# The low parts of the second feed-forward's weights are made partly by GpSimd instead of VectorE

## The reference

```python
    def _L1_ffn_ref(x, w_g, c_fc, c_proj):
        ...
        capacity = max(MIN_CAPACITY, int(CAP_FACTOR * N * TOP_K / E))
        xf = x.reshape(N, C)
        logits = xf @ w_g.T
        top_logits, top_idx = jax.lax.top_k(logits, TOP_K)
        router_probs = jax.nn.softmax(top_logits, axis=-1)
        ...
        h = jnp.einsum('ecd,edf->ecf', buf, c_fc)
        h = jnp.square(jax.nn.relu(h))
        expert_out = jnp.einsum('ecf,efd->ecd', h, c_proj)
        ...
    x = x + 0.5 * _L0_ffn_ref(_layernorm(x, axis=-1), ...)
    x = x + _L0_attn_ref(_layernorm(x, axis=-1), ...)
    x = x + 0.5 * _L0_ffn_ref(_layernorm(x, axis=-1), ...)
    x = x + 0.5 * _L1_ffn_ref(_layernorm(x, axis=-1), w_g, c_fc, c_proj)
    x = x + _L1_attn_ref(_layernorm(x, axis=-1), ...)
    x = x + 0.5 * _L1_ffn_ref(_layernorm(x, axis=-1), w_g, c_fc, c_proj)
```

## Time and profile before

| | |
|---|---|
| median of 3 runs | 3040.18 us (3038.32 to 3042.1) |
| the profiled execution's own time | 3041.84 us |
| its span, first to last instruction | 3040.1 us |
| PE busy | 2598.1 us (85%) |
| DVE busy | 2307.1 us (76%) |
| ACT busy | 2223.2 us (73%) |
| POOL busy | 1637.9 us (54%) |

### The profile page before, as it was taken

How to read it: one execution, slowest core, us unless ns; L and a number is a source line. 1 busy time by engine, 2 the same in 40 slices (tenths; PEclk the granted TensorE clock), 3 DMA queues, 4 the chain that set the end, 5 groups by cost and what they waited for, 6 DMA issues and landing times. The chain is left out here.

```text
span 3040.1 us, 42347 instructions
## 1 busy us (share of the span) xinstructions
PE 2598.1 (85%) x12208; PEld 1727.1 (57%) x12208; DVE 2307.1 (76%) x4329; ACT 2223.2 (73%) x2497; POOL 1637.9 (54%) x1288
## 2 busy tenths in 40 slices
PE   7999979999799996999975878778687777589998
PEld 6877756666587774878852323223232232268887
DVE  7677756777566777898977788787787877498887
ACT  5555536656455555777849999999999999777776
POOL 4667642122266763545536676776756667334444
PEclk9999979999899997999976667766666767689999
DMA  3111111111111112111100000000000000021111
GB/s 134 42 56 41 41 23 41 44 43 43 51 42 56 41 41 96 45 43 45 51 0 1 1 1 1 0 1 1 1 1 1 1 1 1 22 92 56 42 55 42
DMA packets 24917, 101.62 MB, mean 33 GB/s; under 512 B 5856, under 2 KB 7904, under 8 KB 15680
## 3 DMA queue, kind: packets, MB, share of 16 engines
q1 hardware_dynamic: 23360, 99.51, 9.5%
q10 hardware_dynamic: 1408, 0.34, 0.0%
HBM read 82.33 MB, written 2.62 MB: 28 GB/s over the span
## 5 line engine op out<-in xcount | busy, mean ns | idle before, releaser
L1911 POOL TENSOR_TENSOR A_Y<-A_Y,A_U 128x2048 f32<-128x2048 f32 x86 | 390.0, 4558 | 222.1 <-ACT A_U L1958 222.1
L1994 DVE TENSOR_SCALAR A_U<-ps 128x1024 f32<-128x1024 f32 x256 | 309.0, 1217 | 127.0 <-POOL A_Y L1911 58.1
L2000 DVE SCALAR_TENSOR_TENSOR A_U<-ps,A_U 128x1024 f32<-128x1024 f32 x256 | 310.8, 1214 | 57.3 <-PE ps L2144 57.3
L2144 PE MATMUL ps<-A_QT,A_KT 9*128 9x512 f32 x512 | 180.8, 702 | 193.6 <-DVE A_U L2000 162.0
L477 POOL TENSOR_TENSOR F0b_h<-F0b_h,dn 128x512 f32<-128x512 f32 x128 | 212.0, 1661 | 111.9 <-DVE F0b_h L409 111.8
L477 POOL TENSOR_TENSOR F0a_h<-F0a_h,dn 128x512 f32<-128x512 f32 x128 | 212.1, 1662 | 104.6 <-DVE F0a_h L409 104.5
L2144 PEld LDWEIGHTS ps<-A_QT,A_KT 9*128 9x128 f32 x512 | 65.7, 252 | 329.6 <-DVE A_U L2000 237.4
L1911 POOL TENSOR_TENSOR dn<-dn,A_U 128x2048 f32<-128x2048 f32 x42 | 190.3, 4551 | 112.8 <-ACT A_U L1958 112.8
L1958 ACT ACTIVATE A_U<-A_U 128x2048 f32<-128x2048 f32 (+1 forms) x96 | 236.5, 2464 | 0.0
L2116 PE MATMUL ps<-A_Y,A_VA 128*32 128x512 f32 x688 | 228.9, 799 | 5.8 <-DVE A_OT L1893 3.0
L1350 DVE CUSTOM_DVE_ANT_0 ps<-ps,A_mask 128x256 f32<-128x256 f32 (+1 forms) x512 | 184.8, 421 | 58.6 <-PE ps L1430 57.8
(11 more groups left out here) (417 smaller groups left out, 8134.7 us busy)
## 6 DMA issues: line engine op xcount, KB each, us to landing
dn<-weight_rows SPq DMA_DIRECT2D x32, 1024.0 KB, 4.6
F1a_cwb<-weight_rows SPq DMA_DIRECT2D x16, 1024.0 KB, 4.6
F1b_cwb<-weight_rows SPq DMA_DIRECT2D x16, 1024.0 KB, 4.6
A_KZ<-A_KT SPq DMA_DIRECT2D x132, 48.0 KB
A_QZ<-A_qs SPq DMA_DIRECT2D x96, 64.0 KB, 2.0
dn<-in_down SPq DMA_DIRECT2D x2, 2048.0 KB, 12.2
stage<-in_up SPq DMA_DIRECT2D x1, 2560.0 KB, 13.8
X<-in_x SPq DMA_DIRECT2D x4, 512.0 KB, 7.0
```

Of the source, the lines that this page charges most:

```text
L1911: eng.tensor_tensor(flat(y_slot(m, h)), flat(y_slot(m, h)), flat(Um[:, h % UR]), ALU.add).then_inc(s["t_ready"], 1)
L1994: eng.tensor_scalar(u_step(n), d_pair(n), 0.0, None, ALU.max).then_inc(s["dp_vector"], 1)
L2000: eng.scalar_tensor_tensor(out=u, in0=g_pair(), scalar=CLAMP, in1=u, op0=ALU.min, op1=ALU.mult).then_inc(s["u_ready"], 1)
L2144: last = eng.matmul(ps[:, 4 + b, :], KT[r:r + 9, pair, kt * P:(kt + 1) * P], QT[r:r + 9, pair, :], start=True, stop=True)
```

## The change

In both F1 phases VectorE makes the low part of only the front half of the up weights (2048 numbers per partition). GpSimd makes that of the back half, and of all down weights (4096), each behind a `gate_gpsimd`, as soon as ScalarE has made the top parts. A second semaphore, `rest_made_pool`, counts GpSimd's two pieces; TensorE waits for both counters before the first up product, and for GpSimd's second piece before the first down product. Phases F0a and F0b do what they did. The arithmetic is the same.

```diff
-        TOPS, RESTS = (0, 2, 4, 7), (0, 1, 2, 4)
+        TOPS, RESTS, RESTS_POOL = (0, 2, 4, 7), (0, 1, 2, 3), (0, 0, 0, 2)
+        rest_made_pool = sem("rest_made_pool")
...
                 if j == 0 and done == 0:
-                    eng.wait_ge(rest_made, RESTS[number] + 1 + lay)
+                    if lay == 0:
+                        eng.wait_ge(rest_made, RESTS[number] + 1)
+                    else:
+                        eng.wait_ge(rest_made_pool, RESTS_POOL[number] + 2)
...
+                    front, back = slice(0, U1 * HID1 // 2), slice(U1 * HID1 // 2, U1 * HID1)
...
                             eng.wait_ge(rest_made, RESTS[number] + 1)
+                            eng.wait_ge(rest_made_pool, RESTS_POOL[number] + 1)
...
                         if lay == 1:
                             eng.wait_ge(top_made, TOPS[number] + 2)
-                            eng.tensor_tensor(w_rest, w_raw, w_top.bitcast(F32), ALU.subtract).then_inc(rest_made, 1)
-                        eng.wait_ge(top_made, TOPS[number] + 2 + lay)
-                        eng.tensor_tensor(dn_lo[:, :, :, :], dn_raw[:, :, :, :], dn_hi[:, :, :, :].bitcast(F32),
-                                          ALU.subtract).then_inc(rest_made, 1)
+                            eng.tensor_tensor(w_rest[:, front], w_raw[:, front], w_top[:, front].bitcast(F32),
+                                              ALU.subtract).then_inc(rest_made, 1)
                         if lay == 0:
+                            eng.wait_ge(top_made, TOPS[number] + 2)
+                            eng.tensor_tensor(dn_lo[:, :, :, :], dn_raw[:, :, :, :], dn_hi[:, :, :, :].bitcast(F32),
+                                              ALU.subtract).then_inc(rest_made, 1)
                             gated_vector(eng, s, h, hl, nxt)
...
                             eng.drain().then_inc(restart_ready, 1)
+                            eng.wait_ge(top_made, TOPS[number] + 2)
+                            gate_gpsimd(eng)
+                            eng.tensor_tensor(w_rest[:, back], w_raw[:, back], w_top[:, back].bitcast(F32),
+                                              ALU.subtract).then_inc(rest_made_pool, 1)
+                            eng.wait_ge(top_made, TOPS[number] + 3)
+                            gate_gpsimd(eng)
+                            eng.tensor_tensor(dn_lo[:, :, :, :], dn_raw[:, :, :, :], dn_hi[:, :, :, :].bitcast(F32),
+                                              ALU.subtract).then_inc(rest_made_pool, 1)
```

## The result

The changed kernel takes 3063.29 us (median of 4 runs, 3060.17 to 3066.54) against 3040.20 of the kernel before: a ratio of 1.0076, 95% interval 1.0059 to 1.0093. It is 23 us slower. The profiled execution took 3064.49 us with a span of 3062.8.

What follows compares the result with a forecast made beforehand. TensorE's loop was taken to bound the kernel, so a later start moves the end equally. Delays of +11.0 us in F1a and +10.8 in F1b sum to +21.8: 3040.2 + 21.8 = 3062.0, range 3048 to 3067.

Steps and rivals of the forecast that it cites:

- The step that a later start moves the end by as much: F1 loops: TensorE is busy 246.67 of 250 us, so a start x us later moves the kernel's end by x.
- Holding: GpSimd and VectorE, both reading two SBUF operands: whoever is first holds the other for a whole instruction, then the waiter goes.
- Where the pieces fall: F1 starts: back half holds L592 (F1a 3.8 us); down weights hold L596, so F1a's `cw` is at 1197.6, not 1184.80.
- The terms: First activation block, L446 before the change: +11.0 us in F1a, +10.8 us in F1b, sum +21.8 us.
- What no row showed: Whether L592, a `scalar_tensor_tensor`, is held; and `cwb`'s landing time: 4.2 gives 0.8 us less, 6.8 gives 4.4 more.
- The first: Routing, both F1 phases: GpSimd's second piece gets in one or two instructions later; +16.6 us, 3056.8; chance 0.15.
- The second: F1 starts: VectorE keeps the way between its own instructions, so its routing and front half run first; +8.4, 3048.6; chance 0.13.
- The third: F1 starts: GpSimd's pieces run beside VectorE's, nothing is held; only 1.2 us gained, 3039.0; chance 0.06.
- More than computed: TensorE before its fifth block: a clock falling back in the wait, or a late landing, adds some us; 3067 and above; 0.04.
- A sign that was put wrongly: Both F1 phases: TensorE was to be idle some 15 us before the first up product instead of 4.67.

Runs made afterwards that it cites:

- Writing without reading: Against the changed kernel, GpSimd writes zeros into the same two places, each twice, instead of subtracting, so it reads nothing; 3042.51 us, +0.2 against the kernel before.
- the pieces kernel: Against the changed kernel, GpSimd's two subtractions are cut into 4 and 8 of 512 numbers; 3054.73 us, +13.8 against the kernel before.
- the run behind the routing: Against the changed kernel, GpSimd begins its two pieces only when VectorE has made the first activations' low part; 3054.51 us, +12.2 against the kernel before.

## Why the prediction was right

**What bounds the kernel.** The step that a later start moves the end by as much held: the two starts make 20.6 of 23.1 us, and in all eight rows of the table the time follows the starts within 4 us.

**Holding.** It was read from four rows and was the cause. Writing without reading (+0.2 us) shows that the loss needs GpSimd's reading; the pieces show that it is held per instruction. One detail of the reading was too narrow. The prediction says that both must read two operands of SBUF, but two of its own four rows show other forms. L230 is a cast and reads one; casts also hold VectorE (in the kernel before, an L432 issued at 1203.85, just behind a cast of 0.61 us at 1203.80, took 1.10 us). And L1862 on VectorE, a `tensor_scalar`, reads one tensor: in A1 it was issued seven times during a GpSimd addition, took 1.9 to 2.4 us and ended 0.02 to 0.04 us behind it each time, while the same operation elsewhere takes 0.17:

```profile
104.39 0.17 DVE L135 TENSOR_SCALAR var_eps<-mv 128x4 f32<-128x4 f32 x1
```

For the forecast this made no difference, since the instructions that it lays on top of each other do read two. Which one-operand instructions of VectorE are held, these runs don't sort out.

**Where the pieces fall.** The changed kernel's rows have the order that was worked out: back half over the `scalar_tensor_tensor` pair, down weights over the instruction that writes `cw`. The back half was forecast to end 4.85 us after the gate's start and did so after 4.86 (1182.70 to 1187.56).

**The terms.** L450 was forecast 11.0 and 10.8 us late and was, counted from the pair, 10.44 and 10.18 late (1205.06 - 1183.75 = 21.31 against 10.87; 21.05 against 10.87). In F1a the second piece began 0.48 us behind the first and not 0.85, because the gate was held for 0.15 us (it took 0.34, alone 0.19) and not for 0.4, and it took 8.80 us and not 9.05. From the end of L600 to L450 it took 7.76 us, 7.65 expected. These errors make the starts 1.2 us less than the sum; some 2 us outside the starts were not in it. That the median of 3063.29 lies only 1.3 us from 3062.0 is therefore in part luck: the two cancel, and the same kernel measured again gave 3059.21, or +18.3 us where +21.8 was computed.

**What no row showed.** The pair was held (4.43 us), so a `scalar_tensor_tensor` is not exempt. The landing was near the median: L450 started 4.70 and 4.78 us behind the issue of its transfer, 4.6 assumed.

**The rivals.** The first came true in one start of four: the order at the second piece hangs on 0.1 to 0.2 us, and one in four neither confirms nor refutes the chance of 0.15. It accounts for 1.3 us of the difference between the two profiled executions (10.19 against 8.9). The second, VectorE keeping the way between its own instructions, fell too. In the changed kernel the second piece got in between the pair and L600, and once between L600 and L978; there a drain stands between. The pieces kernel shows it without one. The two instructions of the pair have no drain between them, and the second was issued at 1182.47, before the first had ended at 1182.55; all the same a GpSimd piece went between them, and the second took 1.49 us where two take 0.76:

```profile
1182.47 1.49 DVE L596 SCALAR_TENSOR_TENSOR F1a_cwb<-F1a_cwb 128x256 f32<-128x256 f32 x1
```

```profile
1182.23 1.45 POOL L1005 TENSOR_TENSOR up_lo<-F1a_h,up_hi 128x512 fp32r<-128x512 f32 x1
```

The third, no holding, fell.

**More than computed.** The clock's part was small in the changed kernel: in F1a TensorE took 5.3 us for its first twelve matmuls (1200.61 to 1205.87) and not 4.5, but L450, which waited for `cwb`, let it go on no earlier. It is larger where TensorE was stopped in the middle: in the pieces kernel the way from the first to the last down product is 1.8 and 2.1 us longer. Of the last 2 us of the changed kernel none can be laid to the change: the stretch from F1a's last down product to F1b's pair, where half of them lie (1.0 us), differs by up to 5 us between the nine profiles, and single executions of one kernel differ by 2 to 7 us.

**A sign that was put wrongly.** TensorE was to stand idle some 15 us before the first up product. It stood 2.53, because the transposes of `cw` come late as well and lie between; the missing time is in front of them, 18.3 us against 6.2 in the kernel before.

## What to carry to other kernels

When work is moved from VectorE to GpSimd, look at what VectorE does meanwhile and not at how busy GpSimd is. Where VectorE reads two operands of SBUF and GpSimd reads SBUF, the two ran one after the other wherever they met in the rows here, and a long GpSimd instruction holds the next such instruction of VectorE, be it the smallest and most awaited of the kernel. VectorE instructions with one input in PSUM went on beside it (L450), and the memsets on GpSimd, which only write, held nobody. Here 13.3 us of GpSimd work relieved VectorE of 6.6 us that mostly hid behind a transfer, and cost 10 us in each phase, because a short instruction on the chain that decides the start stood behind it. Nor does the earliest start of the added work help: in the run behind the routing GpSimd began 5.4 us later, and the loss was +12.2 us, against +18.3 and +23.1 of the changed kernel. Held time shows as long rows of the engine that is held, so compare the duration of the same small instruction in both profiles; and where a piece must go to GpSimd, start it behind the chain, cut it, or defer it on VectorE to where it has idle time.

## What the hardware showed beyond this

- TensorE's lower clock level (granted clock 0.50, 1.2 GHz) lasted longer in some restarts. In F1a of the kernel before, after 4.67 us of idle time, matmuls followed each other every 0.43 us for 3.1 us and then every 0.23. In the changed kernel, in F1a, after transposes and 2.53 us of idle time that had followed 18.3 us of it, this lasted some 5.7 us (0.50 from 1200.60 to 1206.20, 1.00 behind it); in F1b 4.4.
- A wait in the middle of the loop's start had different effects. After 3.81 us TensorE went at its lower level for 5.2 us (the pieces kernel, F1a). With only the down weights on GpSimd it went at it at once after 2.35 us in F1a (granted 0.50 from 1198.40 to 1201.50). In F1b, after 3.42 us, it did five matmuls at the higher level and then fell, while busy (granted 1.00 from 2688.70 to 2689.80, 0.50 from 2690.00 to 2692.50). In the run behind the routing it did not fall in F1b after 3.15 us (1.00 from 2694.30 to 2698.00). What decides isn't shown by these runs.
- A GpSimd instruction on one number per partition took 2.83 us, nearly all of it waiting for a VectorE instruction of 4.42 us; as a gate it tells in the trace how long the way was closed.
- The order of two engines at one place changed between executions of the same kernel when ScalarE, behind a transfer, was 0.08 us later, and with it which instruction paid 9 us.
